# Local layers of a macaron block: 64-row scores, the query's cosine product moved to GpSimd, and half of the diagonal blocks moved by DMA

## What is computed

```python
def attn_layer(x, Wqkv, qs, ksc, Wo):            # 16 heads of 64, windows of 32 tokens
    q, k, v = split(x @ Wqkv)
    q = l2norm(q) * qs
    k = l2norm(k) * ksc
    q = q * cos * scale + rotate_half(q) * sin * scale
    k = k * cos * inv + rotate_half(k) * sin * inv
    # each window of 32 queries sees its own 32 keys and the 32 before
    attn = softmax(mask(q @ look(k).T * 8))
    return (attn @ look(v)) @ Wo

for i in range(6):
    x = attn_layer(shift_tokens(x), ...) + x
    x = ffn_layer(shift_tokens(x), ...) + x      # layer norm, W1, gelu gate, W2
```

## Time and profile before

| what | us |
|---|---|
| median of 3 runs | 4699.27 (4692.64 to 4707.0) |
| profiled execution, its own time | 4695.61 |
| its span, first to last instruction | 4693.8 |
| PE busy | 4058.7 (86%) |
| DVE busy | 3754.1 (80%) |
| ACT busy | 3051.5 (65%) |
| POOL busy | 2034.4 (43%) |
| mean granted TensorE clock | 0.953 of full |

### The profile page before, as it was taken

One profiled execution on the slowest core, in us unless ns is written; L12 is line 12 of the kernel. 1 busy time (PEld: TensorE's weight loads), 2 busy tenths in 40 slices (PEclk: granted clock), 3 DMA queues, 4 the chain that ended last, 5 costly groups with the idle time before them and its releaser, 6 DMA issues. The chain is left out here.

```text
span 4693.8 us, 116229 instructions
## 1 busy us (share of the span) xinstructions
PE 4058.7 (86%) x42352; PEld 3115.0 (66%) x42352; DVE 3754.1 (80%) x7533; ACT 3051.5 (65%) x4888; POOL 2034.4 (43%) x1420
## 2 busy tenths in 40 slices
PE   5988988989989889938858689899899898898898
PEld 4866857857758768616535478578577587686685
DVE  7988979979979889845335389799799798798897
ACT  5866857848848758612413478488488487586685
POOL 5544536535536545320010155265355365354452
PEclk9999999999999999967968899999999999999999
DMA  1000000000000000040030000000000000000000
GB/s 51 9 24 14 8 31 7 9 29 9 23 14 9 22 17 8 6 95 2 1 81 2 25 17 9 30 8 8 28 9 23 14 9 22 15 9 24 13 8 13
DMA packets 30619, 88.78 MB, mean 19 GB/s; under 512 B 7504, under 2 KB 13648, under 8 KB 28368
## 3 DMA queue, kind: packets, MB, share of 16 engines
q1 hardware_dynamic: 29104, 80.95, 6.4%
q10 hardware_dynamic: 1152, 3.15, 0.3%
HBM read 38.72 MB, written 1.05 MB: 8 GB/s over the span
## 5 line engine op out<-in xcount | busy, mean ns | idle before, releaser
L780 POOL TENSOR_TENSOR pool<-pool 128x512 f32<-128x512 f32 x768 | 1177.1, 1563 | 1147.0 <-DVE pool L878 1147.0
L450 PE MATMUL psum<-squares,pool 128*128 128x128 f32 x3072 | 710.0, 278 | 66.3 <-POOL pool L784 35.6
L452 PE MATMUL psum<-squares,pool 128*128 128x128 f32 x3072 | 700.2, 275 | 0.0
L492 PE MATMUL psum<-wqkv_hi,xs_lo 128*128 128x512 f32 x1152 | 514.0, 446 | 110.4 <-DVE pool L878 45.5
L867 DVE TENSOR_REDUCE pool<-pool 128x16 f32<-128x1024 f32 x384 | 453.4, 1216 | 177.9 <-ACT pool L694 174.6
L483 PE MATMUL psum<-pool 128*64 128x128 f32 x6144 | 539.5, 289 | 61.7 <-ACT pool L670 54.7
L655 ACT COPY pool<-psum 64x512 f32<-64x512 f32 x768 | 447.3, 582 | 215.2 <-PE psum L452 209.9
L450 PEld LDWEIGHTS psum<-squares,pool 128*128 128x128 f32 x3072 | 432.7, 141 | 149.3 <-issue 61.1
L670 ACT COPY pool<-pool 32x512 f32<-32x512 f32 x768 | 486.7, 634 | 9.0
L694 ACT ACTIVATE pool<-psum 128x1024 f32<-128x1024 f32 x384 | 376.5, 1023 | 171.6 <-PE psum L494 167.7
L493 PE MATMUL psum<-wqkv_lo,xs_hi 128*128 128x512 f32 x1152 | 461.7, 401 | 0.0
(11 more groups left out here) (167 smaller groups left out, 8172.0 us busy)
## 6 DMA issues: line engine op xcount, KB each, us to landing
pool<-pool SPq DMA_DIRECT2D x192, 128.0 KB, 2.3
pool<-in_wqkv SPq DMA_DIRECT2D x12, 1536.0 KB, 6.1
k_st<-turn_st SPq DMA_DIRECT2D x8, 1536.0 KB, 21.4
pool<-in_wo SPq DMA_DIRECT2D x12, 512.0 KB, 3.5
pool<-in_w SPq DMA_DIRECT2D x12, 341.0 KB, 3.0
pool<-in_w SPq DMA_DIRECT2D x12, 192.0 KB, 2.8
rotary<-in_rotary SPq DMA_DIRECT2D x2, 1024.0 KB, 5.1
pool<-in_scale SPq DMA_DIRECT2D x12, 128.0 KB, 6.6
```

The source lines that it names most:

```text
L450: pe.matmul(o, by_cos[:, p // 2, 2 * c:2 * c + 2, :], ident, start=True, stop=False, is_transpose=True)
L452: last = pe.matmul(o, by_sin[:, p // 2, 2 * c:2 * c + 2, :], ident, start=False, stop=True, is_transpose=True)
L492: pe.matmul(o, xs_lo[:, k % 2, :], wqkv_hi[:, c], start=True, stop=False)
L780: last = g.tensor_tensor(by_sin[:, q, :, hd * r:hd * r + hd], qn[:, q, :, hd * (1 - r):hd * (2 - r)], tab, ALU.mult)
```

## The change

Four edits, all in the local layers:

- **Scores.** `kT` has one set of columns for both heads of a pair, so the two heads differ only by the half of the partitions on which they stand. Each matmul contracts 64 rows and has 64 columns; there are 64 of them a unit instead of 32. The heads stand in another order in the scores (all even ones, then all odd ones), and the value matmuls pick them accordingly. ACT copies each k group once, on 128 partitions; POOL's `keep` moves half as much.
- **Cosine.** POOL makes both cosine products, each right after its sine; DVE's L888 is gone. `cos_ready` counts two a unit, and `k_cos_ready` is gone.
- **Diagonal.** ACT copies the blocks of windows 0 and 1 (with `pT_last`, four copies). Those of windows 2 and 3 are moved by four DMAs a unit, issued by SP. They count on a new semaphore, `pt_sent`; PE's values and DVE's next block transposes wait for it too.
- **SP's order.** In each step SP first does the diagonal of U-2 and then the `v_last` copy. After the loop it does the last two diagonals, and only then waits for the last sine and cosine and loads the next projections.

```diff
+        def pt_by(unit):
+            return (unit + 1) * 16 * NW + CREDIT
...
-            kT = [cut(PAIRS, 2, WIN + P) for _ in range(2)]
+            kT = [cut(PAIRS, WIN + P) for _ in range(2)]
...
+                        def diagonal(U):
+
+                            sp.wait_ge(block_ready, done(U))
+                            plain(sp)
+                            sp.wait_ge(o_ready, done(U - 1))
+                            plain(sp)
+                            for w in range(NW // 2, NW):
+                                rows = slice(WIN * w, WIN * w + WIN)
+                                sp.dma_start(pT[WIN * (w - 1):WIN * w, :, rows],
+                                             turned_P[rows, :, 0:WIN]).then_inc(pt_sent, 16)
+                                sp.dma_start(pT[rows, :, rows], turned_P[rows, :, WIN:2 * WIN]).then_inc(pt_sent, 16)
+
                         def step(i, k, has):
 
                             U = U0 + 4 * i + k
+                            if has(2):
+                                diagonal(U - 2)
...
                         attention(sp, step)
+                        diagonal(U0 + UNITS - 2)
+                        diagonal(U0 + UNITS - 1)
...
                                 if c % 4 == 0:
                                     pe.wait_ge(t_out, done(U, 4, 2 + c // 4))
+                                    plain(pe)
                                 for w in range(NW):
-                                    o = bank(4 + c // 4)[WIN * w:WIN * w + WIN, P * (c % 4):P * (c % 4) + P]
-                                    last = pe.matmul(o, qT[:, c, WIN * w:WIN * w + WIN],
-                                                     kT[k % 2][:, c, :, WIN * w:WIN * w + 2 * WIN],
-                                                     start=False, stop=(c % 4 == 3))
+                                    for r in range(2):
+                                        rows = slice(64 * r, 64 * r + 64)
+                                        o = bank(4 + r)[WIN * w:WIN * w + WIN, 2 * WIN * c:2 * WIN * c + 2 * WIN]
+                                        last = pe.matmul(o, qT[rows, c, WIN * w:WIN * w + WIN],
+                                                         kT[k % 2][rows, c, WIN * w:WIN * w + 2 * WIN],
+                                                         start=False, stop=(c == PAIRS - 1))
...
                             pe.wait_ge(pt_ready, done(U))
+                            pe.wait_ge(pt_sent, pt_by(U))
...
-                                for r in range(2):
-                                    last = a.copy(kT[k % 2][64 * r:64 * r + 64, c:c + 4, r, WIN:WIN + P],
-                                                  bank(7 - p % 2)[64 * r:64 * r + 64, :]
-                                                  .rearrange("p (c t) -> p c t", c=4))
-                                last.then_inc(t_out, 1)
+                                a.copy(kT[k % 2][:, c:c + 4, WIN:WIN + P],
+                                       bank(7 - p % 2).rearrange("p (c t) -> p c t", c=4)).then_inc(t_out, 1)
...
-                            for w in range(NW):
+                            for w in range(NW // 2):
...
-                                tab = turn[:, bass.ds(t, 1), 1, :].broadcast_to([P, HEADS, DH])
-                                g.tensor_tensor(by_cos[:, 1], qn[:, 1], tab, ALU.mult).then_inc(k_cos_ready, 1)
+                                    tab = turn[:, bass.ds(t, 1), q, :].broadcast_to([P, HEADS, DH])
+                                    g.tensor_tensor(by_cos[:, q], qn[:, q], tab, ALU.mult).then_inc(cos_ready, 1)
...
                                     v.wait_ge(pt_ready, done(U - 1))
+                                    v.wait_ge(pt_sent, pt_by(U - 1))
...
-                                if k == 0:
-                                    v.wait_ge(turn_ready, done(l + L0))
-                                v.wait_ge(qn_ready, done(U, 2, 1))
-                                v.wait_ge(t_ready, done(U - 1, 4, 1))
-                                tab = turn[:, bass.ds(t, 1), 0, :].broadcast_to([P, HEADS, DH])
-                                v.tensor_tensor(by_cos[:, 0], qn[:, 0], tab, ALU.mult).then_inc(cos_ready, 1)
```

More of the change, by code:

```diff
@@ L61, in macaron_program @@
         sq_ready, qn_ready, cos_ready = sem("sq_ready"), sem("qn_ready"), sem("cos_ready")
-        k_cos_ready = sem("k_cos_ready")
         sin_ready, turn_ready = sem("sin_ready"), sem("turn_ready")
@@ L65, in macaron_program @@
         k_kept, s_ready, s_taken, p_ready = sem("k_kept"), sem("s_ready"), sem("s_taken"), sem("p_ready")
-        block_ready, pt_ready = sem("block_ready"), sem("pt_ready")
+        block_ready, pt_ready, pt_sent = sem("block_ready"), sem("pt_ready"), sem("pt_sent")
         o_ready, o_out, wo_ready, y_ready = sem("o_ready"), sem("o_out"), sem("wo_ready"), sem("y_ready")
@@ L90, in macaron_program @@
         gout_made, gx_added, go_clear = sem("gout_made"), sem("gx_added"), sem("go_clear")
-        passed_sp, passed_pool = sem("passed_sp"), sem("passed_pool")
+        passed_sp, passed_pool, passed_pe = sem("passed_sp"), sem("passed_pool"), sem("passed_pe")
         counted = {
@@ L96, in macaron_program @@
                        rb_ready, w1_ready, w2_ready],
-            "scalar": [xs_ready, sq_ready, v_out, t_out, p_ready, pt_ready, o_out, fsq_ready, gel_ready],
-            "vector": [qn_ready, cos_ready, s_taken, block_ready, y_ready, norm_step, soft_step,
+            "scalar": [xs_ready, sq_ready, v_out, t_out, p_ready, pt_ready, pt_sent, o_out, fsq_ready, gel_ready],
+            "vector": [qn_ready, s_taken, block_ready, y_ready, norm_step, soft_step,
                        xc_ready, diag_ready, xn_ready, hid_ready, x_ready, var_step, aff_step],
-            "gpsimd": [lo_ready, w_hi, w_split, sin_ready, k_cos_ready, turn_ready, k_kept],
+            "gpsimd": [lo_ready, w_hi, w_split, sin_ready, cos_ready, turn_ready, k_kept],
         }
@@ L123, in plain @@
         def plain(eng):
-            eng.sem_inc(passed_sp if eng is nc.sync else passed_pool, 1)
+            eng.sem_inc(passed_sp if eng is nc.sync else passed_pe if eng is nc.tensor else passed_pool, 1)
         def rsqrt(v, x, tmp, step, first, op0, c0, op1, c1, between=()):
@@ L312, in tables @@
             def tables(eng, layer):
-                eng.wait_ge(cos_ready, done(layer * UNITS - 1))
-                eng.wait_ge(k_cos_ready, done(layer * UNITS - 1))
+                eng.wait_ge(cos_ready, done(layer * UNITS - 1, 2, 1))
                 eng.wait_ge(sin_ready, done(layer * UNITS - 1, 2, 1))
@@ L406, in _ @@
                         sp.wait_ge(sin_ready, done(last, 2, 1))
-                        plain(sp)
-                        sp.wait_ge(cos_ready, done(last))
-                        sp.wait_ge(k_cos_ready, done(last))
+                        sp.wait_ge(cos_ready, done(last, 2, 1))
                         plain(sp)
@@ L433, in turned_scores @@
                             pe.wait_ge(sin_ready, done(U, 2, 0))
-                            pe.wait_ge(cos_ready, done(U))
+                            pe.wait_ge(cos_ready, done(U, 2, 0))
                             if isinstance(i, int) and i == 0 and k == 0:
@@ L443, in turned_scores @@
                                     pe.wait_ge(sin_ready, done(U, 2, 1))
-                                    pe.wait_ge(k_cos_ready, done(U))
+                                    pe.wait_ge(cos_ready, done(U, 2, 1))
                                 if p >= 2:
@@ L480, in values @@
                             for h in range(HEADS):
-                                r = 64 * (h % 2)
+                                r, at_h = 64 * (h % 2), PAIRS * (h % 2) + h // 2
                                 o = bank(6 + h // 8)[r:r + 64, P * (h // 2 % 4):P * (h // 2 % 4) + P]
-                                pe.matmul(o, V[k % 4][:, DH * h:DH * h + DH], pT[:, h, :], start=True, stop=False)
+                                pe.matmul(o, V[k % 4][:, DH * h:DH * h + DH], pT[:, at_h, :], start=True, stop=False)
                                 last = pe.matmul(o[:, 0:WIN], v_last[k % 2][:, DH * h:DH * h + DH],
-                                                 pT_last[:, h, :], start=False, stop=True)
+                                                 pT_last[:, at_h, :], start=False, stop=True)
                             last.then_inc(o_ready, 1)
@@ L761, in keep @@
                             plain(g)
-                            g.tensor_copy(b[:, :, :, 0:WIN], b[:, :, :, P:P + WIN]).then_inc(k_kept, 1)
+                            g.tensor_copy(b[:, :, 0:WIN], b[:, :, P:P + WIN]).then_inc(k_kept, 1)
                         def step(i, k, has):
@@ L862, in step @@
                             if has(0):
-                                t = 2 * i + k // 2
                                 for q in range(2):
@@ L874, in step @@
                                 v.wait_ge(sin_ready, done(U - 1, 2, 1))
```

(3 more changed lines are left out.)

## The result

The changed kernel took 4728.8 us (median of 13 runs), the kernel before 4701.7 us beside it: ratio 1.0057, 95% interval 1.0039 to 1.0075. It is slower by 0.6%, where 4655 us was forecast. Lines of this kernel have moved: L878 is now L894, L145 and L146 are L148 and L149, L780 and L784 are L797 and L801, L469 is L488, L483 is L503, L492 is L512, L833 is L851, L926 is L936.

What follows compares the result with a forecast made beforehand. A tight ring of PE, DVE and ACT, with POOL's instructions holding DVE, was taken as the bound. Loops +31, ends -10 x 7.1 and -2 x 1.9 gave -44 us: 4655 us, own range 4620 to 4710.

Steps and rivals of the forecast that it cites:

- Either way it is hidden.: 64-row scores on PE: 128 passes take 1.0 to 1.9 us, covered because POOL's last cosine holds PE.
- A: DVE's first norm instruction arrives later than 7.7 us, waits for POOL's last cosine: unit 16.5 us, 4748 us; chance 0.16.
- rival C: Diagonal DMAs land after more than 11.4 us and decide the ring: unit 17.8 us, 4966 us; chance 0.06.
- D: Layer end: weight preparation meets as much DVE work in the feed-forward part as before: about 4707 us; chance 0.05.
- POOL's chain and DVE behind it: Local-layer unit: POOL's 10.05 us chain holds DVE's next norm; unit 15.95 us against 16.02, loss 31 us in all.
- rival B: POOL does not hold DVE, so the trades work: unit about 14.3 us, 4356 us; chance 0.07.
- In the loop this is cover gained and no time: ACT loses 2.5 us of diagonal and about 1.2 us of key copies a unit; no time gained, POOL's chain decides.
- Transfers: Diagonal DMAs take 5.1 us from block_ready to pt_sent (4.2 to 13.3); PE's values wait 1.2 us, covered.
- Ends: Layer ends: later weight loads unblock DVE; gain 7.1 us in ten layers with weights, 1.9 in two without.
- The issue gap: PE's scores: by the skill page's about 25 ns, 128 passes would take 3.2 us, where 1.0 to 1.9 was taken.

Runs made afterwards that it cites:

- the written-out run: The changed kernel with TensorE's attention loop of three rounds written out three times, other engines keeping their loop: 4612.9 us, ratio 0.9796 to the kernel before.
- C and D: The changed kernel with the old 128-row scores and key copies, cosine on POOL and diagonals by DMA kept, loop not written out: 4670.3 us, ratio 0.9935.
- S and D: The changed kernel, TensorE's attention loop written out, with the query cosine on VectorE again (64-row scores and diagonals by DMA kept): 4567.1 us, ratio 0.9720.
- C: The part that moves the query's cosine product to POOL; never run alone. It cost 101 us on 64-row scores, 63 on DMA diagonals, 46 on both.
- S alone: The kernel before with only the 64-row scores and their key copies, TensorE's attention loop written out: 4599.0 us, ratio 0.9780.
- D on S: Diagonals by DMA with SP's new order, added to the 64-row scores with TensorE's attention loop written out: 4567.1 us against 4599.0 without them.
- D alone: The kernel before with only half of the diagonal blocks by DMA and SP's new order, loops as they were: 4607.6 us, ratio 0.9808.

## Why the prediction was wrong

**The step that failed** is that of the 64-row scores: "Either way it is hidden." It priced the doubled number of score matmuls as time on PE (1.0 to 1.9 us; it took 1.6) and not as code. They bring the round from 1,637 to 2,160 recorded instructions (1,568 to 2,083 matmuls and weight loads), past what PE kept, and that cost 4729 - 4613 = 116 us. No rival held it: A, C and D put a slower kernel down to L145, the transfers or the weights. Without it the change gains 88 us (4700.7 to 4612.9), so the sign would have been right. The number would not have been much better founded: 4613 lies 42 us under the forecast, because the loops came out 51 us shorter than in its sum (2797, not 2848) and the ends 17 us longer (785, not 768).

The other steps, against the written-out run, where the code plays no part:

- **POOL's chain and DVE behind it: right in kind.** POOL 10.05 us forecast; L148 at 6.65 us after the first L878's end; L149 waits to 10.15. In the timeline of a unit of the written-out run, L148 comes at 841.36 and L149 ends at 844.86, with the first L899 from 833.57 to 834.75: 6.6 and 10.1 us. But only 69 of the 168 inner units of that run wait there (15.8 us on average); in 92 it is L156 that waits (15.5 us), and the mean is 15.7, under the forecast's own 15.85 to 16.1. The unit with C and D, the old scores kept, averages 15.9 us as the 15.95 said, but as a mean of units of 15.7 (L156 waits) and 16.1 (L149 waits), so the match is in part luck; rival B is out.
- **"In the loop this is cover gained and no time" (ACT): wrong.** S and D give 2814 - 2755 = 59 us in the loops once C is left out, 77 with S alone, and the 0.81 us wait for ACT is gone there. The prediction had read that wait, but counted with it only for the moment at which L145 arrives, where POOL's chain swallowed it. With C in place most of it is eaten by the hold: 2797, where the working of the prediction had 2848. What C does was sized at +31 us by itself; it costs 42 to 78 in the loops.
- **Transfers: late, and covered behind POOL's chain.** The way is 6.9 us, not 5.1, within the bounds; PE waits up to 3.0 us for them. A wait over 2 us was named as the sign of rival C; it came, but the units stayed at 15.5 to 15.8 us, far from C's 17.8. Without C the transfers are not free: D on S adds 18 us to the loops.
- **Ends: right in kind, too large by 1.7 to 2.6 us of 7.1.** The weights come where they were forecast, 1008.36 - 971.62 = 36.7 us after the last L894 (37 forecast), and the rotation table (L319, before L317) holds DVE at the second chunk's deviation, 3.9 us (4.5 forecast). L308 also holds L921 for 2.0 us, which the sum did not have:

```profile
1008.36 2.75 POOL L308 CAST wqkv_hi<-pool 128x3072 fp32r<-128x3072 f32 x1 [24.78 <-DMA pool<-in_scale]
1008.81 2.57 DVE L921 TENSOR_SCALAR pool<-pool 128x512 f32<-128x512 f32 x1
...
1016.87 4.53 POOL L319 TENSOR_TENSOR pool<-rotary,pool 128x2048 f32<-128x2048 f32 x1
1017.57 3.86 DVE L153 TENSOR_SCALAR pool<-pool 128x4 f32<-128x4 f32 x1
```

  Gain per end 4.5 us in the changed kernel, 5.4 written out, instead of 7.1; with D alone it is 6.8.
- **The issue gap.** 128 passes in 1.61 us are 12.6 ns each. The Trainium skill, page "TensorE: Matmul & The Clock Gate", section "Back-to-back issue gap", has about 25 ns; the trace does not agree for these passes, and the estimate of 3.2 us from it falls.

What stays open: which limit PE's code store has (it lies between rounds of 1,637 and 1,900 recorded instructions), which engine's jump back costs most at a layer's start (the four were written out together), and why C costs more on S than on S and D.

## What to carry to other kernels

- Count instructions as code, not only as time. For each loop ask whether a whole round still fits in what the engine keeps; the DMA rows of instruction packets tell: a loop that fits has next to none from its second round on. Splitting one matmul in two can push a loop over the edge, and the price stands elsewhere, at the jump back.
- Where a loop does not fit, write it out: here that turned a loss of 0.6% into a gain of 2.0%, though as much code is fetched as before. Where it fits, writing it out was worth nothing.
- A busy engine that others wait for 0.8 us each unit is not cover. And a product moved from DVE to POOL is no relief when POOL's instructions hold DVE's next ones.

## What the runs showed of the hardware

- PE kept the code of a round of 1,637 recorded instructions (1 instruction packet in 130 us over the second and third round), and fetched one of 1,900 afresh (17 packets). Each jump back then idles 2.9 to 4.6 us, and at 22 to 23 of 24 of them the granted clock is 0.51 (1.2 GHz) for 3.4 or 6.8 us around its end. Written out, the changed kernel fetches as much (18 packets) and does not idle.
- The Trainium skill, page "Runtime: NRT & Kernel Launch", section "Instruction fetch mechanics", gives TensorE room for 2,048 instructions, filled in blocks of 256, and says that a taken branch to code outside it waits for a fetch. The trace agrees with the wait. The round of 1,900 recorded instructions misses already, so less than the whole room was to be had for a loop here.
- DVE's tensor_scalar from SBUF to SBUF waits for a running POOL instruction: L149 takes 1.83 us where it takes 0.2 at the least, and ends with POOL's cosine (883.01 and 882.97). A reduction is not held: the two L884 (876.94 to 879.28) run beside POOL's products and take 1.2 us each, as they do elsewhere.
- Score passes of 64 rows and 64 columns on alternating parts of the array follow each other every 12.6 ns, those of 128 rows and 128 columns every 31 ns.
